# Norm, key and query projections and values of three attention layers in one block, keys first

## What is computed

```python
def layer(x, ctx):                         # x = x + layer(layernorm(x), ctx)
    q = layernorm(x) @ Wq.T + bq           # L3x: Wk and bk here too
    k = ctx @ Wk.T + bk                    # L2x: no biases
    v = ctx @ Wv.T + bv
    q, k = rope(q), rope(k)                # L2x only: t * cos + rotated(t) * sin
    scores = q @ k.T * scale               # by head
    scores = where(mask == 0, -1e9, scores)            # L0x and L3x
    # L3x only: exp(sigmoid(pdiff)), |i-j| and -softplus(gammas) fade the scores
    #   total_effect = clip(exp(sqrt((tot - cum) * pos) * gamma * diff), 1e-5, 1e5)
    return softmax(scores) @ v @ Wo.T + bo
```

## Time and profile before

| | |
|---|---|
| time, median of 3 runs | 3425.42 us (3422.04 to 3426.59) |
| the profiled execution, its own time | 3424.7 us |
| its span, first to last instruction | 3422.8 us |
[...]
| front of L0x, start to first score | 120.6 us |
| front of L2x | 106.9 us |
| front of L3x | 108.6 us |

### The profile page before, as it was taken

How to read it: one execution, slowest core, us unless ns; L and a number is a source line. 1 busy time by engine, 2 the same in 40 slices (tenths; PEclk the granted TensorE clock), 3 DMA queues, 4 the chain that set the end, 5 groups by cost and what they waited for, 6 DMA issues and landing times. The chain is left out here.

```text
span 3422.8 us, 48765 instructions
## 1 busy us (share of the span) xinstructions
PE 2789.1 (81%) x14898; PEld 1568.8 (46%) x14992; DVE 1958.6 (57%) x4849; ACT 1730.3 (51%) x2836; POOL 804.4 (24%) x911
## 2 busy tenths in 40 slices
PE   5899849969999997657699799998667777777777
PEld 2333249934444444323222359996324343343443
DVE  6577641155555555107788521114678888888853
ACT  2366511136555554101377423331469889889953
POOL 2000020020000000001100030003357777777740
PEclk8899969979999999788899999999779999999998
DMA  4111136520000000892122239994410000000001
GB/s 159 38 52 45 46 128 209 197 85 1 1 1 1 1 1 15 354 425 77 60 57 61 85 145 351 345 343 136 155 19 19 19 21 13 25 18 9 25 24 51
DMA packets 160959, 326.54 MB, mean 95 GB/s; under 512 B 29360, under 2 KB 128432, under 8 KB 137136
## 3 DMA queue, kind: packets, MB, share of 16 engines
q1 hardware_dynamic: 156208, 312.13, 26.1%
q0 software_dynamic: 4608, 12.59, 1.1%
HBM read 275.22 MB, written 49.28 MB: 95 GB/s over the span
## 5 line engine op out<-in xcount | busy, mean ns | idle before, releaser
L3135 DVE TENSOR_TENSOR_SCAN L3x_fade<-L3x_first_exp,L3x_scores 128x513 f32<-128x513 f32 x256 | 311.5, 1217 | 48.1 <-PE L3x_probs_tp L2945 47.0
L3016 POOL TENSOR_TENSOR L3x_fade<-L3x_fade,L3x_apart 128x1024 f32<-128x1024 f32 x128 | 278.9, 2179 | 196.6 <-DVE L3x_mx L3153 157.7
L2942 PE MATMUL L3x_probs_tp<-identity,L3x_fade 128*128 128x128 f32 x1024 | 163.6, 283 | 177.4 <-ACT L3x_probs_T L3081 143.6
L1430 ACT ACTIVATE L1x_probs<-L1x_scores,L1x_neg_max 128x512 f32<-128x512 f32 x256 | 173.5, 683 | 226.6 <-DVE L1x_neg_max L1484 226.6
L2942 PEld LDWEIGHTS L3x_probs_tp<-identity,L3x_fade 128*128 128x128 f32 x1024 | 113.9, 142 | 281.2 <-issue 140.2
L1484 DVE TENSOR_REDUCE L1x_neg_max<-L1x_scores 128x2 f32<-128x1024 f32 x128 | 156.7, 1224 | 142.9 <-PE L1x_scores L1319 142.9
L1824 ACT ACTIVATE L2f_hiddenT<-L2f_hidden_ps,L2f_b1s 128x128 f32<-128x128 f32 x320 | 99.9, 363 | 208.3 <-PE L2f_hidden_ps L1759 208.3
L3053 ACT ACTIVATE L3x_first_exp<-L3x_scores,L3x_nm 128x512 f32<-128x512 f32 x256 | 175.4, 685 | 54.2 <-DVE L3x_nm L3127 52.6
L930 DVE CUSTOM_DVE_ANT_0 L0x_masked_scores<-L0x_s,L0x_mask_q 128x512 f32<-128x512 f32 x256 | 167.0, 685 | 57.6 <-issue 57.5
L3061 ACT ACTIVATE L3x_fade<-L3x_fade,L3x_tiny,L3x_rl 128x512 f32<-128x512 f32 x256 | 194.4, 814 | 0.0
L925 DVE TENSOR_REDUCE L2x_neg_max<-L2x_s 128x1 f32<-128x512 f32 x256 | 164.7, 685 | 36.5 <-PE L2x_s L819 36.0
(11 more groups left out here) (522 smaller groups left out, 6174.9 us busy)
## 6 DMA issues: line engine op xcount, KB each, us to landing
L2f_w1s<-in_L_w SPq DMA_DIRECT2D x40, 1024.0 KB, 7.5
L2f_w2s<-in_L_w SPq DMA_DIRECT2D x40, 1024.0 KB, 6.4
L1f_w1s<-in_L_w SPq DMA_DIRECT2D x32, 1024.0 KB, 16.0
L1f_w2s<-in_L_w SPq DMA_DIRECT2D x32, 1024.0 KB, 10.7
L0f_w1s<-in_L_w SPq DMA_DIRECT2D x16, 1024.0 KB, 6.1
L0f_w2s<-in_L_w SPq DMA_DIRECT2D x16, 1024.0 KB, 5.2
L0x_q_stack<-L0x_q_parts SPq DMA_DIRECT2D x96, 64.0 KB, 2.4
L0x_k_stack<-L0x_k_parts SPq DMA_DIRECT2D x96, 64.0 KB, 2.5
```

The source lines that it names most:

```text
L1430: nc.scalar.activation(p[:, n % 3, h, :], s[:, n % 2, h, :], ACT.Exp, bias=nmax[:, n % 4, h:h + 1], accum_out=den[:, n % 4, h:h + 1]).then ...
L2942: nc.tensor.matmul(tp[:, kt, :], fz[:, f, kt * P:(kt + 1) * P], c.ident[:], start=(kt == 0), stop=False, is_transpose=True)
L3016: nc.gpsimd.tensor_tensor(fz[:, f:f + 2, 0:S], fz[:, f:f + 2, 0:S], w, ALU.mult).then_inc(y_done, 1)
L3135: nc.vector.tensor_tensor_scan(fz[:, f, :], ex[:, t, :], sA[:, t, 0:1].to_broadcast([P, S + 1]), 0.0, ALU.add, ALU.bypass).then_inc(f_done, 1)
```

## The change

The five blocks of a front become one block, `norm_and_project`, and the blocks of the heads behind it. `load_resident`, `layer_norm`, `project_split`, `project_values`, `prepare_all_masked`, and the unused `attention` are gone.

- All 8 jobs of the keys come first, as they need only the context; then the 16 tiles of values, with the tile of x_normed behind each on VectorE; then, batch by batch, two turns of x_normed, their copies, and two jobs of queries.
- A job without rotation: ScalarE evicts it twice, to `full`, which now lies in PSUM with two buffers, and as the leading part to SBUF. VectorE subtracts (one input in PSUM) and casts the middle part. With rotation: GpSimd multiplies by cosine, VectorE multiplies by sine and adds in PSUM, ScalarE casts the leading part; the split of job j-1 is behind the addition of job j on VectorE.
- Semaphores for the loads of keys, values and queries are separate. ScalarE's queue issues x (L0x), the masks and the tables of L3x; SP issues the weights, the context in four slices, and behind them the identity.
- Statistics of x in L0x lie between the splits of the last four key jobs, before the variance.
- Sums of values: GpSimd adds the four tiles of a batch (12 additions), TensorE has one matmul for each batch. GpSimd sets the ones and zeros.
- L3x: sigmoids and two exponents lie behind the keys on ScalarE, the other exponents and the products between query jobs; the set of activation tables with exponent and logarithm is asked for behind the sigmoids.
- The stacks of heads 0 to 7 are loaded from SP behind the last six query jobs, four transfers each. The two row sets of ones are still set in the next block.

The loops over heads, the feed-forward parts and L1x are not changed.

```diff
-def load_resident(c):
+def resident_opening(c):
...
+    def context(sp):
+        ctx = dram["ctxT"].rearrange("(k p) t -> p k t", p=P)
+        for n in range(B):
+            sp.dma_start(c.ctxT[:, :, n * S:(n + 1) * S], ctx[:, :, n * S:(n + 1) * S]).then_inc(c.ctx_loaded[n], 16)
+        sp.dma_start(c.ident[:], dram["ident"]).then_inc(ident_loaded, 16)
...
+    def statistics(dve, n):
+        if n == 0:
+            dve.wait_ge(ident_loaded, 16)
             nc.vector.tensor_copy(c.identb[:], c.ident[:])
+        dve.wait_ge(x_loaded[n], 16)
+        for t in range(n * TB, n * TB + TB):
+            nc.vector.bn_stats(c.stats[:, t, :], c.x[:, t, :])
...
+def norm_and_project(c, owner, ctx, tag, stacks, loads, k_loaded, v_loaded, q_loaded, weights, biases, scale, dest, vaug, vw,
+                     prepare=None, rope=None, masked=None, beside=None, opening=None):
...
             @block.sync
             def _(sp):
+                loads[0](sp)
+                if opening:
+                    opening[0](sp)
+                loads[1](sp)
+                for j, (_, m, b, _, _, _, d) in enumerate(jobs):
+                    sp.wait_ge(lo_done, j + 1)
...
+                    sp.dma_start(to, parts[:, j % R, :, :]).then_inc(stored[j % R], 16)
+                    if j == NK + 2:
+
+                        sp.wait_ge(stored[0], 16 * (1 + NK // R))
+                    if j >= NK + 2:
+                        n = j - (NK + 2)
+                        stacks.load(sp, 0, n // 3, range(n % 3 * 2, n % 3 * 2 + 2))
...
+                pe.wait_ge(*k_loaded)
+                for j in range(NK):
+                    if opening and j % MT == 0:
+                        pe.wait_ge(c.ctx_loaded[j // MT], 16)
+                    project(j)
+                    if rope and j:
+                        rotate(j - 1)
+                pe.wait_ge(*v_loaded)
+                for t in range(NT):
+                    values(t)
+                    if rope and t == 0:
+                        rotate(NK - 1)
+                pe.wait_ge(*q_loaded)
+                for i in range(NT // 2):
+                    turn(i)
+                    if i % 2:
+                        pe.wait_ge(turn_free, i + 1)
+                        for j in range(NK + i // 2 * MT, NK + (i // 2 + 1) * MT):
+                            project(j)
+                            if rope and j > NK:
+                                rotate(j - 1)
+                        if masked and i in (3, 5):
+                            value_sums(i - 3)
...
+                def take(j):
...
+                    wait_pos(act, rest_done, j - 1)
+                    evict(full[:, j % 2, :]).then_inc(full_done, 1)
+
+                    wait_pos(act, stored[j % R], 16 * (j // R))
+                    one = evict(parts[:, j % R, 0, :])
+                    one.then_inc(acc_read, 1)
+
+                def leading(j):
+
+                    act.wait_ge(full_done, j + 1)
+                    wait_pos(act, stored[j % R], 16 * (j // R))
+                    nc.scalar.copy(parts[:, j % R, 0, :], full[:, j % 2, :]).then_inc(hi_done, 1)
...
+                loads[2](act)
+                if not opening:
+                    root()
+                act.wait_ge(*k_loaded)
+                for j in range(NK):
+                    take(j)
+                    if rope and j:
+                        leading(j - 1)
...
+                for i in range(NT // 2):
+                    act.wait_ge(turned, i + 1)
+                    nc.scalar.copy(c.xnT[:, :, i * 2 * P:(i + 1) * 2 * P],
+                                   tp[:, i % 2, :].rearrange("p (k t) -> p k t", k=KD)).then_inc(turn_free, 1)
+                    if i % 2:
+                        for j in range(NK + i // 2 * MT, NK + (i // 2 + 1) * MT):
+                            take(j)
+                            if rope and j > NK:
+                                leading(j - 1)
+                        if beside and i in (1, 3):
+                            beside.exponents(act, 2 + i // 2)
...
+                def turn_by_angle(j):
+                    d = jobs[j][6]
+                    dve.wait_ge(rot_done, j + 1)
+                    nc.vector.tensor_tensor(full[:, j % 2, :], full[:, j % 2, :], sin[:, d, :], ALU.mult
+                                            ).then_inc(bys_done, 1)
+                    dve.wait_ge(byc_done, j + 1)
+                    dve.wait_ge(bys_done, j + 1)
+                    nc.vector.tensor_tensor(full[:, j % 2, :], full[:, j % 2, :], byc[:, j % R, :], ALU.add
+                                            ).then_inc(full_done, 1)
...
+                for j in range(NK):
+                    if opening and j >= TB:
+                        opening[2](dve, j - TB)
+                    if rope:
+                        turn_by_angle(j)
+                        if j:
+                            split(j - 1)
+                    else:
+                        split(j)
...
+                for j in range(NK, NJ):
+                    if rope:
+                        by_cos(j)
+                        if j > NK:
+                            last_part(j - 1)
                     else:
+                        last_part(j)
+                    if beside and j == NK + 1:
+                        beside.pool_product(pool, 0)
...
-                load_group(0, 0, None)
-                load_group(0, 1, None)
                 load_group(0, 2, 8)
                 load_group(0, 3, 16)
```

More of the change, by code:

```diff
@@ new lines, in norm_and_project @@
+def norm_and_project(c, owner, ctx, tag, stacks, loads, k_loaded, v_loaded, q_loaded, weights, biases, scale, dest, vaug, vw,
+                     prepare=None, rope=None, masked=None, beside=None, opening=None):
+    nc = c.nc
+    dk, R = 16, 4
+    HD = H * dk
+    MT = HD // P
+    W = H * vw
+    wq, wk, wv = weights
+    bq, bk, bv = biases
+    c.xn = c.sb(owner, tag + "x_normed", [P, NT, D], F32)
+    c.xnT = c.sb(owner, tag + "x_normed_T", [P, KD, N], F32)
+    stats = c.stats
+    jobs = [(wk, m, b, c.ctxT, bk[:, m:m + 1] if bk is not None else None, 1.0, 1) for b in range(B) for m in range(MT)]
+    jobs += [(wq, m, b, c.xnT, bq[:, m:m + 1] if bq is not None else None, scale, 0) for b in range(B) for m in range(MT)]
+    NJ, NK = len(jobs), B * MT
@@ new lines, in _ @@
+                act.wait_ge(*k_loaded)
[3 more added lines that the diff above has]
+                        leading(j - 1)
+                if rope:
+                    leading(NK - 1)
+                if opening:
+                    root()
+                if beside:
+                    beside.sigmoids(act)
+                    beside.exponents(act, 0)
+                    beside.exponents(act, 1)
+                if bq is not None:
+                    act.wait_ge(ready, 1)
@@ L282, in _ @@
+                if rope:
+                    split(NJ - 1)
+                if beside:
+                    beside.product(dve, 3)
+                    beside.gamma_end(dve)
             @block.gpsimd
             def _(pool):
-                with pool.Fori(0, B) as b:
-                    for j in range(NJ):
-                        n = b * NJ + (j + 1)
-                        pool.wait_ge(mid_done, n)
-                        nc.gpsimd.tensor_tensor(parts[:, j % R, 2, :], rest[:, j % R, :], parts[:, j % R, 1, :],
-                                                ALU.subtract).then_inc(lo_done, 1)
@@ L775, in load_group @@
                 def load_group(b, hg, wait):
-                    half = hg % 2
-                    if wait is not None:
-                        sp.wait_ge(s2_done, wait)
-                    for st, parts, src in ((qst, QB, qs), (kst, KB, ks)):
-                        for i, part in enumerate(parts):
-                            sp.dma_start(st[i * dk:(i + 1) * dk, 4 * half:4 * half + 4, :],
-                                         src[part, 4 * hg * dk:4 * (hg + 1) * dk, ds(b * S, S)].rearrange(
-                                             "(h r) t -> r h t", r=dk)).then_inc(group_loaded[half], 16)
+                    sp.wait_ge(s2_done, wait)
+                    stacks.load(sp, b, hg)
                 def store_batch(b, par):
@@ L3253, in store_output @@
+        distance_attention(c, tag, stacks, vaug, o_dram, (mq, am, vsum, row_mask), apart, gamma)
+    project_out(c, tag, HD, o_dram, "L3_woT", "L3_bo")
 def store_output(c, out):
```

1012 lines of the change are left out of this document (345 added, 667 removed).

## The result

The changed kernel takes 3407.95 us (median of 6 runs, 3402.63 to 3410.99) against 3426.01 (6 runs, 3422.04 to 3434.11), a ratio of 0.9936 with a 95% interval of 0.9925 to 0.9947. It is faster, by 18 us and not by the 56 forecast, and outside the range of 3347 to 3391. The span of the profiled execution went from 3422.8 to 3404.6 us, the granted clock over it from 0.932 to 0.933.

What follows compares the result with a forecast made beforehand. In the fronts of L0x, L2x and L3x no engine is busy three quarters of the time; stages with different limits run in a row. L0x -38.5, L3x -27, L2x +9.5 make -56: 3425.4 to 3369.4 us, range 3347 to 3391.

Steps and rivals of the forecast that it cites:

- the ring of L2x: L2x front: GpSimd and VectorE wait for each other in turns, 4.3 us a job against 3.8; front +9.5 us.
- the borders: L2x queries: at three batch borders, 6.2 us from addition to addition, through ScalarE's copies queued behind the leading cast.
- the ring did close: Its opposite was a rival: GpSimd has slack, L2x runs at 3.4 us a job, 3353 us in all; chance 0.15.
- the slow clock: Rival with chance 0.03; a granted clock of 0.8 or more was named as a sign of the forecast being right.
- something came of the change: Its opposite was a rival: no gain, as the first heads then wait for something else; chance 0.02.
- Queues and ports: Rival for L0x and L3x: GpSimd holds x_normed and key stores land late; 3387 us, chance 0.17.
- the 5 that were named as a sign: L3x front: key stores landing after 5 us or more would show the forecast wrong.
- On attention loops behind the fronts ... I count nothing: Head loops behind the fronts: taken as unchanged; a difference of more than 3 us would show the forecast wrong.
- The norm of a tile (0.41) fits beside: L0x values: VectorE's x_normed, 0.41 us a tile, fits beside TensorE's 0.86 a tile; values take 12 to 14 us.
- The tail: End of a front: 7 us from last matmul to landed store, then in L0x 4.8 us of the next block.
- the 1.7 allowed for handovers: L0x front: the terms came to 80.3 us and 82 was taken, to allow for handovers.
- The issuing on ScalarE: L3x front: ScalarE's issuing of loads holds back its square root and first eviction; 12 us, bounds 3.2 and 13.

Runs made afterwards that it cites:

- e5: Changed kernel with GpSimd in L2x making the cosine product of job j before the last part of job j-2; ratio 0.9936 to the kernel before.
- e4: Changed kernel with GpSimd's additions of value tiles in L0x on 8 columns instead of 512; ratio 0.9940 to the kernel before.
- e8: Changed kernel with x_normed of L0x made by ScalarE instead of VectorE, GpSimd's additions kept; ratio 0.9927 to the kernel before.
- e7: Changed kernel with ScalarE issuing L0x's masks and L3x's distance, gamma and mask behind the seventh key job; ratio 0.9928 to the kernel before.
- e6: Changed kernel with VectorE reading the sums of values one job earlier in L0x and L3x; ratio 0.9930 to the kernel before.
- e1: Changed kernel with 64 one-column memsets more on VectorE in the L3x front; ratio 0.9905 to the kernel before.
- e2: Changed kernel with 128 one-column memsets more on VectorE in the L3x front; ratio 0.9949 to the kernel before.

## Why the prediction was wrong

**The direction and the ring of L2x were right.** The front of L2x: 116.5 us forecast, 116.5 measured, with 4.25 us between additions for 4.3, VectorE waiting for GpSimd, and 6.04 at the borders for 6.2. Its ring came out of following who is queued behind whom, and e5 confirmed it. That the sum came out to the tenth is luck: the terms as written add up to 116.7, the keys took 28.0 us from first to last addition for 30.1, since the ring closes only from the third job on, the first addition began at 14.0 for 15, and the values took 16.5 for 13. Of the rivals, the ring did close, the granted clock stayed at 0.85 to 0.91 in the fronts, against the slow clock that had 0.03 of the chances, and something came of the change. The subtraction from PSUM took 0.69 us, as forecast, for 1.37 before. *Queues and ports* (0.17, 3387) was nearest: it has GpSimd's additions hold x_normed in L0x (+8), and the key stores of L3x land late beside ScalarE's loads (+10 beyond the 3 of the forecast). The first half is true (+7 for +8). The second is true in kind and not in size, and no run shows its +10: the first four key stores of L3x landed after 6.6 us, past the 5 that were named as a sign, but that cost ScalarE 4.0 us, about the 3 already allowed (the keys ended at 29.9 us for 29.5). Even so its 3387 is 21 us too low.

**"On attention loops behind the fronts ... I count nothing" is the step that failed most, +13.1.** The prediction named it as what would make it wrong, but gave it no price and no chance. The view that could have warned is the table of DMA queues, which has rows of instruction packets (q14: 64 in the kernel before, 91 after), beside a change that moves every loop behind it in every stream. Over the middle of the loop the trace has 26 packets of 8 KB (0.21 MB) and 15.6 us of issue waits for 2 packets and none, three packets at each back jump. That these packets are VectorE's code, brought in anew in every turn, is inferred from their coming and going with its waits. The same loop has both waits at 0 and +128 and one of them at -16, and neither at -91, +44 and +64. Why these places differ no run shows.

**"The norm of a tile (0.41) fits beside" failed, 7 us of front (e4, e8).** The values took 20.0 us for 13; 4.6 of these 7.0 go with the hold (e4), the other 2.4 stay without it, at a granted clock of 0.89. The 0.41 of the earlier trace rows was measured while GpSimd was idle, so it couldn't tell whether GpSimd holds the operation. I took it as if it could. The trace of after has up to 1.16 us beside an addition, 0.40 without. What I should have read was the earlier trace rows, where a subtraction between two SBUF tiles takes 1.37 us beside GpSimd, twice the 0.68 of other operations on 512 columns.

**Other terms of L0x.** Keys ended at 33.6 us for 27 (+6.6): the loads kept the DMA engines busy throughout from 2 to 26 us, at 358 GB/s in the mean, where I had looked at the first 7 us alone; the first job began at 9.5 for 7, and the identity, at the end of the queue, held the first statistics to 22.3 for 16. Only 2 of it came back in e7; that an earlier identity would bring more wasn't tried, so the cause of this term is argued and not shown. The queries took 29.2 us for 26.4, since reading the sums of values is queued behind a split (e6 took 3.6 off). The tail was right (12.5 for 11.8). Keys 6.6, root 0.3, values 7.0, queries 2.8 and tail 0.7, less the 1.7 allowed for handovers, come to 15.7, for the 15.6 by which this front is off.

**L3x, +5.1** (the terms as written add up to 81.2 and not to 81.5). Keys and values ended where forecast (29.9 and 44.0 us for 29.5 and 43.5). The queries were 3.1 longer: behind the waits for two exponents on ScalarE (3.25 and 2.33 us) TensorE came back at a granted clock of 0.70 and 0.68, and the two jobs behind each took 5.25 and 5.40 us together, for 3.70 at 1.00. The tail was 1.8 longer; no run shows why. The issuing on ScalarE was sized right, 11.9 us for 12, and with what it did to the stores it was worth 3.7 to 5.4 (e7).

## What to carry to other kernels

A change that adds or removes instructions moves every loop behind it. Where the profile's instruction queue has packets in a loop and "issue" waits stand behind its back jump, the price is paid in each turn (3.1 us here); try a few tens of cheap instructions in a gap of that engine before anything else is blamed. A duration read while the other engine is idle says nothing of contention: look for a row with both at work. And when two engines hand work to each other in turns, follow the ring through the orders of both, then look for the next ring just behind it.

## What the runs showed of the hardware

- The loop over heads took 774 us or 787 us with the same instructions, by its place in VectorE's stream alone; at -16 it took 781 to 783, with one of the two waits.
- x_normed of L0x wasn't held where it began before GpSimd's addition: the one at 43.33 took 0.41 us with an addition beginning 0.16 us later, as in five more cases of this trace, and 1.16 when the addition had begun 0.26 us before it. The held ones ended about 0.15 us after the addition, with 0.26 to 0.70 us of it gone at their start.
- The granted clock behind an idle stretch, in the kernel before: the first 8 matmuls of the values of L0x, behind 16.7 us without work for TensorE, took 3.78 us at 0.50 (78 to 82 us), the other 56 took 12.35 us at 1.00 (82 to 96), 0.88 for each tile.
- The end of the L3x heads, from the last scan to the output projection, took 49 to 51 us in most profiles and 59 in e1 and e7, where the profiled execution was the slowest of its kernel (3438 and 3444 us, medians 3426 and 3436). In e1 the granted clock was 0.63 over 36 us of it, in e2 0.89 over the same stretch. Nothing in the kernels differs there; why the clock fell stays open.

```profile
3310.00:3346.00 36.00, 22.40 (x114) 12.64 (x115) 3.35 (x15) 5.73 (x10) 1.29 (x6) 0.63 0.16 44
```

```profile
3310.00:3344.00 34.00, 19.89 (x132) 11.53 (x132) 5.39 (x23) 7.48 (x13) 3.78 (x15) 0.89 0.15 47
```
